# Loading and splitting the weights of experts 2 and 3 later in a routed mixture-of-experts kernel

## The reference

```python
c = einsum('btd,od->bto', x, W) + scale_b * (x @ A_b.T) @ B_b.T      # conditioned rows, [1024, 256]
logits = c @ w_gate.T                                                # 8 experts
top_w, top_i = top_k(softmax_integer(logits), 2); top_w /= top_w.sum(-1)
for e in range(8):                                                   # w1, w3: [8, 704, 256], w2: [8, 256, 704]
    h = silu(c @ w1[e].T) * (c @ w3[e].T)
    out = out + combine[:, e:e + 1] * (h @ w2[e].T)
return x + out
```

## Time and profile before

| what | value |
|---|---|
| time, median of 3 runs | 213.94 us (209.70 to 224.81) |
| span of the profiled execution | 203.8 us |
| granted TensorE clock, mean over the span | 0.990 |
| PE busy | 95% of the span |
| POOL busy | 66% |
| DVE busy | 52% |
| ACT busy | 40% |

### The profile page before, as it was taken

One profiled execution on the slowest core, in us unless ns is written; L12 is line 12 of the kernel. 1 busy time (PEld: TensorE's weight loads), 2 busy tenths in 40 slices (PEclk: granted clock), 3 DMA queues, 4 the chain that ended last, 5 costly groups with the idle time before them and its releaser, 6 DMA issues.

```text
span 203.8 us, 3875 instructions
## 1 busy us (share of the span) xinstructions
PE 194.4 (95%) x1209; PEld 170.6 (84%) x1209; DVE 106.3 (52%) x307; ACT 82.5 (40%) x224; POOL 134.7 (66%) x115
## 2 busy tenths in 40 slices
PE   7799999699999999999999999999999999999992
PEld 6487998588778998899889988998889888988871
DVE  0568899683433454345334533453666344434484
ACT  2467484277653433243323332333234323432560
POOL 8300088787899968999999999999143474016600
PEclk9889999999999999999999999999999999999999
DMA  5999994499769993356436518202411121001915
GB/s 138 400 367 339 302 392 182 106 330 413 290 207 323 349 339 127 129 151 213 129 59 244 171 42 253 88 3 48 183 55 64 43 72 60 26 29 32 360 48 207
DMA packets 21634, 37.25 MB, mean 183 GB/s; under 512 B 2416, under 2 KB 14960, under 8 KB 21488
## 3 DMA queue, kind: packets, MB, share of 16 engines
q1 hardware_dynamic: 18080, 30.15, 44.8%
q0 software_dynamic: 1984, 5.25, 7.0%
q10 hardware_dynamic: 1552, 1.61, 2.4%
HBM read 25.45 MB, written 11.54 MB: 182 GB/s over the span
## 4 chain that ended last, share of the span: by engine, by line
PE 70%; POOL 9%; DMA 8%; ACT 4%; issue 4%; DVE 2%; SPq 0%; ACTq 0%; DVEq 0%; POOLq 0%
PE gu L1202 23%; PE gu L1211 11%; POOL slot_rows L490 7%; PE ya L1239 6%; PE ht L1218 6%; PE ya L1240 5%; PE ya L1241 5%; DMA x<-x_t 3%; DMA rows<-expert_rows 2%; ACT w_all L582 2%; PE xt L1182 2%; POOL rows L473 2%; DMA slot_rows<-c_rows,pos_i 2%; PE gu L1084 2%; DMA expert_rows<-rows,dst_i 1%
## 5 line engine op out<-in xcount | busy, mean ns | idle before, releaser
L1202 PE MATMUL gu<-w_all,xs_hi 128*128 (+2 forms) x276 | 70.8, 378 | 0.1
L902 DVE TENSOR_TENSOR hid<-gu,sg 128x256 f32<-128x256 f32 x46 | 19.5, 424 | 63.6 <-ACT sg L640 63.6
L1202 PEld LDWEIGHTS gu<-w_all,xs_hi 128*128 128x128 f32 x276 | 46.7, 188 | 4.5 <-issue 0.3
L479 POOL TENSOR_TENSOR w_all<-raw,w_all 128x1024 fp32r<-128x1024 f32 (+2 forms) x15 | 46.9, 3133 | 0.1
L640 ACT ACTIVATE sg<-gu 128x256 f32<-128x256 f32 x46 | 17.7, 384 | 70.5 <-PE gu L1211 70.5
L1211 PE MATMUL gu<-w_all,xs_lo 128*128 (+1 forms) x138 | 40.5, 374 | 0.0
L1239 PE MATMUL ya<-w_all,h_hi 128*128 (+1 forms) x115 | 38.5, 334 | 0.5 <-DVE h_lo L917 0.3
L509 POOL DMA_INDIRECT expert_rows<-rows,dst_i x21 | 20.6, 983 | 27.1 <-DVE rows L923 11.4
L490 POOL DMA_INDIRECT slot_rows<-c_rows,pos_i x16 | 19.3, 1207 | 23.3 <-DVE pos_i L825 18.7
L1240 PE MATMUL ya<-w_all,h_hi 128*128 (+1 forms) x115 | 32.5, 283 | 0.0
L1241 PE MATMUL ya<-w_all,h_lo 128*128 (+1 forms) x115 | 32.2, 280 | 0.0
(11 more groups left out here) (191 smaller groups left out, 268.5 us busy)
## 6 DMA issues: line engine op xcount, KB each, us to landing
raw<-expert_weights SPq DMA_DIRECT2D x6, 896.0 KB, 5.4
raw<-expert_weights SPq DMA_DIRECT2D x6, 640.0 KB, 5.6
raw<-expert_weights SPq DMA_DIRECT2D x6, 512.0 KB, 6.0
slot_rows<-zeros SPq DMA_DIRECT2D x1, 2432.0 KB, 16.4
expert_rows<-zeros SPq DMA_DIRECT2D x1, 2048.0 KB, 13.8
rows<-expert_rows SPq DMA_DIRECT2D x4, 512.0 KB, 5.4
rows<-slot_rows SPq DMA_DIRECT2D x1, 1152.0 KB, 8.3
cond_rows<-c_rows ACTq DMA_DIRECT2D x4, 256.0 KB
```

Source lines behind the costliest of these rows:

```text
L479: return nc.gpsimd.tensor_tensor(lo_part(e, cols), from_raw(e)[:, cols], as_f32(hi_part(e, cols)), ALU.subtract)
L902: nc.vector.tensor_tensor(hid[i % HBUFS][:, :].rearrange("p (a b) -> p a b", b=P), bank[:, :].rearrange("p (a k b) -> p a k b", k=2, b=P)[ ...
L1202: nc.tensor.matmul(out, stay_hi[:, kc * P:(kc + 1) * P], moving(at, part + first + kc * P, n), start=kc == 0 and part == HI_COLS, stop=False)
```

## The change

SP: the second piece of expert 2's raw weights no longer waits for the gather of slot 1. It waits for all 16 sends, and SP issues `slot_rows(0)` right ahead of it. So pieces 2 and 3 and the tail of expert 2, and all of expert 3, are loaded behind these. ACT: only the first piece of expert 2 is still copied at item 3. Its other two pieces are copied at items 12 and 13 in place of 4 and 5, the three pieces of expert 3 at items 14, 15 and 16 in place of 6, 7 and 8. DVE: the four small instructions of `destinations` stand at item 3 in place of item 5, ahead of the last low part of expert 1.

```diff
@@ raw_weights (SP)
                     if e == STAGED + 1 and k == 1:
-                        sp.wait_ge(rows_in[1], 16)
+                        for i in range(2):
+                            sp.wait_ge(c_sent[i], 16 * TOP * FIRST_TILES)
+                        slot_rows(0)
                     sp.dma_start(from_raw(e)[:, cols], w_dram[e, :, cols]).then_inc(landed[k], 16)
@@ SP's program
             raw_weights(1)
-            raw_weights(2)
-            sp.wait_ge(xt_done, 1)
-            raw_weights(STAGED_LOW)
             def slot_rows(g):
...
-            for i in range(2):
-                sp.wait_ge(c_sent[i], 16 * TOP * FIRST_TILES)
-            slot_rows(0)
+            raw_weights(2)
+            sp.wait_ge(xt_done, 1)
+            raw_weights(STAGED_LOW)
             sp.wait_ge(w_ready, STAGED + 1)
@@ ACT, item loop
-                if 3 <= i < 6:
-                    expert_hi(2, i - 3)
-                if 6 <= i < 9:
-                    if i > 6:
-                        act.wait_ge(c_sent[i - 7], 16 * TOP * FIRST_TILES)
-                    expert_hi(3, i - 6)
+                if i == 3:
+                    expert_hi(2, 0)
+                if 12 <= i < 14:
+                    expert_hi(2, i - 11)
+                if 14 <= i < 17:
+                    if i > 14:
+                        act.wait_ge(c_sent[i - 15], 16 * TOP * FIRST_TILES)
+                    expert_hi(3, i - 14)
@@ DVE, item loop
-                if i == 5:
-                    destinations()
...
                 if i == 3:
+                    destinations()
                     expert_lo(1, 2)
                     expert_tail_lo(1).then_inc(w_ready, 1)
```

## The result

| | before | after |
|---|---|---|
| median of the timed runs | 212.97 us (4 runs, 209.70 to 224.81) | 217.25 us (4 runs, 216.52 to 218.17) |
| ratio of the undisturbed runs | | 1.029, 95% interval 1.0245 to 1.0337 |
| span of the profiled execution | 203.8 us | 214.5 us |
| time of the profiled execution | not listed | 216.52 us |

The account below looks back on a forecast made before the run. PE was taken as the bound, with POOL's chain a second bound 2 us under it. A shift of 8.6 less 2.05 slack gave 6.5 us: span 203.8 to 210.3, plus 10.1 offset, 220.4 us; range 215.0 to 225.0.

Parts of the forecast that it names:

- shift of 8.6 us: POOL's whole chain of experts 4 to 7 moves later by 8.6 us, behind expert 4's later weights.
- slack of 2.05: Expert 7's weights ready at 141.21, ahead of item 47's down at 143.34: some 2.05 us, the least of any expert.
- The gain of 1.4 us at item 12: PE reaches item 12 1.4 us earlier: 1.9 of stalls removed less 0.5 for destinations; bounds -0.2 to 1.9.
- destinations, 0.5 us: Four small DVE instructions at item 3 go on PE's path ahead of item 5's down: a loss of 0.5 us.
- POOL gets piece (2,1) at 64.7: POOL stands still after low(2,0) until ACT has copied expert 2's next piece at item 12, done at 64.7 us.
- Expert 4's weights come at 83.6 and bind: Expert 4's first piece lands 8.6 us later, at 83.6; POOL, done with expert 3 at 82.3, waits 1.3 us.
- The offset of 10.1 us: Distance of the median shown, 213.94, over the span of 203.8; added to the forecast span of 210.3.
- The stalls' sum of some 8 us: PE stands waiting for POOL at items 35, 41 and 47, some 8 us together.
- the first: Rival: POOL alone bounds, DMAs in time; shift 6.2, loss 4.1 us, time 218.1 us; chance 0.2.
- The third: Rival: DMA side worse, 339 GB/s, and PE's stalls of about 3 us cost clock; 223 to 225 us; chance 0.12.
- The second: Rival, faster: first slots of experts 5, 6 and 7 each one slot later, PE keeps its gain; 212.5 us; chance 0.05.
- the fourth: Rival, little change: ACT copies piece 2 before item 12, POOL's delay stays small; 214 to 217 us; chance 0.08.

Follow-up runs that it names:

- r_after: The changed kernel, unaltered, run once more for its trace; 217.88 us, span 215.9.
- p_before: The kernel before, unaltered, run once more for its trace; 212.60 us, span 210.6.
- e4: Changed kernel in which POOL subtracts only 8 columns of each piece of expert 4, leaving out part of the computation; 210.74 us, ratio to before 0.993.
- e3: Changed kernel with ACT's copies at items 10 to 14 in place of 12 to 16; 215.48 us, ratio to before 1.017.
- e1: Kernel before with only ACT's copies moved to items 12 to 16, SP's and DVE's order kept; 222.82 us, undisturbed ratio 1.040.
- s2: Kernel before with only the first 8 of POOL's 16 sends, those waiting for the sends waiting for these 8; 215.40 us in one execution.
- s1: Kernel before with 63 more, already satisfied waits in ACT's program ahead of its first copy; 215.44 us in one execution.

## Why the prediction was right, and where not

The direction, the mechanism and the places were right: POOL is a second bound close under PE's, ACT's copy at item 12 stops it, expert 7 comes too late for item 47, and PE stands at items 35, 41 and 47. The time, 217.25, lies in the range and 3.2 us under the 220.4. But the sum reached it in part by errors that cancel, and that is luck. The loss forecast, 6.5 us, is near the measured 5 to 6 (2.9% of before by the ratio, 217.25 - 212.0 by the medians). It was put together from a shift of 8.6 us less a slack of 2.05. In ordinary executions it is a shift of 10.8 to 11.8 us (after, r_after) less a slack of 8.1 (p_before), and 1.4 to 1.6 us of lower clock, which the sum had at nothing: 4.1 and 5.3 us.

- **The gain of 1.4 us at item 12.** About right, as far as can be told: e4's time says 1.3 (0.6 to 2.2). Single traces don't settle it, since their pauses differ: against p_before (68.02), item 12 starts 2.6 us earlier in after, 1.6 in r_after, 1.8 in e4 and 0.8 in e3.
- **destinations, 0.5 us.** Right in kind: item 5's down starts at 46.43 behind slot_out, in place of 46.04, 0.4 us.
- **The copies at items 12 to 16 cost PE nothing.** Right: items 12 to 17 keep PE's pace (67.84 to 77.09 for items 13 to 17, 9.25 us; before 64.59 to 73.81, 9.22).
- **POOL gets piece (2,1) at 64.7.** Wrong by 4.7 us: 69.43. The way from item 12's start to this point was right, 4.0 us (65.42 to 69.43) where 3.9 had been reckoned (60.8 to 64.7). What was wrong is item 12's start: the step took it from the one trace of before, less 1.4, and all the later traces have a pause of ACT and DVE ahead of it.
- **Expert 4's weights come at 83.6 and bind.** The time was about right, as e3 shows (84.75, with the wait of 0.82 ahead of it). The queue started earlier by 0.7 us in after (its load of slots 4 and 5 is issued at 55.76 in place of 56.47) and by 1.8 in r_after (54.63), where 1.1 had been taken, and the stretch from 59 to 84 us moved 354 GB/s in after and 350 in e3, not the 407 that the sum took from a stretch with the sends in it. The prediction's other figure for these bytes, 11.0 us, gives 84.9. That they bind was wrong for the changed kernel: POOL came at 87.1, later than they. The term that was mis-sized is the one above. With the 10.0 and 7.6 us for experts 3 and 2, which held (69.43 to 77.06 to 87.06), POOL alone gives the whole shift.
- **Expert 7 ready at 149.8.** 151.97, and 153.0 in r_after.
- **The slack of 2.05 us.** Together with the offset the largest error. It was read from one quick execution. In p_before it is 8.1 us. The loss by the prediction's own rule is then 151.97 - 149.36 = 2.6 us at item 47's down, plus 0.1 until it starts, 0.6 for its slower matmuls and 0.8 in the item behind it: 4.1, and the two spans differ by 3.9. With r_after it is 153.04 - 149.36 = 3.7 plus 1.6: 5.3, and the spans differ by 5.3.
- **The offset of 10.1 us.** It is 2.0 us. The prediction's own span of 210.3 stood against 214.5. The 4.2 us between them are 2.3 at item 47's down, for which POOL comes later than reckoned, 1.4 for the lower clock (0.6 in that down, 0.8 in item 48) and 0.5 behind it. The 8 us too much in the offset hid them.
- **The stalls' sum of some 8 us** was 6.7 with the clock's part, 7.2 in r_after.

On the rivals: the first (POOL alone is the bound, the DMAs in time) is the one that describes the changed kernel best, with a later start than it assumed. The third was right on one point: behind the stand of 2.8 us the clock fell to 0.50 and cost 0.8 us in the next item (1.6 in r_after), while the stands of 0.6 and 1.35 us left no mark. The second and the fourth fell.

The change has a side that the prediction didn't name. Before, POOL's chain ran from the end of the sends and didn't hang on PE's progress, so that a pause of PE gave POOL slack. With the copies in item 12, POOL starts when PE gets there, and a pause ahead of item 12 delays both alike. From item 12's start to expert 7 ready it is 86.6 us in after (65.42 to 151.97), in r_after (66.43 to 153.04) and in e1 (71.60 to 158.25). From item 12's start to the down of item 47, where POOL doesn't hold PE up, it is 81.2 us, 81.3 in p_before and 81.2 in e4. So in these executions expert 7 is 5.4 us late however long the pause, and the slack that a pause used to give is gone. (Without any pause POOL would be done with expert 3 at an estimated 82.4, by the prediction's own steps, and the DMAs would bind, by the 84.75 of e3; no run shows that case.)

## What to carry to other kernels

Before work is moved later to relieve one engine, follow who waits for it down to the last consumer, and compare the slack there with the whole shift: here at most 1.9 us of stalls on ACT were traded for a shift of 10.8 us in a chain with 8 us of slack. Work that feeds a helper engine's serial chain should hang on data, not on an item of the main loop, or the helper loses its lead whenever the main loop stumbles. And a slack or an offset read from one execution is only as good as that execution: where the span lies far under the median shown, ask for what the ordinary runs have more.

## What the runs showed of the hardware that was not expected

- ACT and DVE pause between about 44 and 58 us in every trace but the first one of before. In nine of these ten traces waits are put down to no recorded event, 5.8 us together on ACT in p_before (1.75 and 4.09) and 1.13 in after, where PE's items 8 and 9 take 8.9 us in place of 4.4; in the tenth, s2, DVE's instructions are long instead. In s1, with 63 more waits in ACT's program, the pause stands at the same item. It doesn't go with half of POOL's sends (s2) or with SP's load traffic (after). A second one of 3.5 to 4 us on ACT ends between 172 and 180 us in nine of the ten (in after at 178.46, in p_before at 174.75) and at 186 in e1, and costs PE 0.5 to 1 us. Their cause is open.
- PE at a granted clock of 0.50 (1.2 GHz) for some 3 us directly behind a stand of 2.8 us, ahead of item 48, and also behind one of 2.45 us in e3 (0.50 from 151 to 154). The same is seen behind the pause: 0.60 from 56 to 60 in p_before. Behind the stands of 0.6 and 1.35 us of after there was none (1.00 from 121 to 124 and from 135.5 to 138.5).
- The distance from span to time is 1.9 to 2.1 us in all the executions of this study for which both are listed, but for the one of s2 with 1.7.
